# A fused four-layer kernel: attention outputs turned in pairs of head groups, elementwise steps given to GpSimd, a new order table

## The reference, cut to what matters

```python
x = x + L0_xattn(layernorm(x), ctx)      # causal, v has a bias
x = x + L0_ffn(layernorm(x))             # sign(weight)
x = x + L1_xattn(layernorm(x), ctx)      # causal
x = x + L1_ffn(layernorm(x))             # 16 experts, top 2, and 2 shared
x = x + L2_xattn(ctx, layernorm(x))      # masked; q, k, v = layernorm(linear) * scale + bias
x = x + L2_ffn(layernorm(x))             # quantised
x = x + L3_xattn(layernorm(x), ctx)      # no weights: k = v = ctx
x = x + L3_ffn(layernorm(x))             # 3 blocks of two quantised low-rank linears

# attention, for each head
weights = softmax(q @ k.T * scale); out = weights @ v
# L2_ffn: both inputs of a product are quantised
scale = 127.0 / clip(max(abs(x)), 1e-05); xq = clip(round(x * scale), -128.0, 127.0) / scale
bitlinear(x, w) = act_quant(x) @ weight_quant(w).T
out = bitlinear(silu(bitlinear(x, w_gate)) * bitlinear(x, w_up), w_down)
# L3_ffn: weight of each linear
w = (q / 7.5 - 1.0) * repeat(scale, 16); y = x @ w.T + bias + (x @ la.T) @ lb.T
```

## Time and profile before

| | us |
|---|---|
| median of 3 runs | 1191.2 |
| lowest, highest run | 1190.59, 1201.41 |
| the profiled execution | 1198.55 |
| its span, first to last instruction | 1196.6 |

### The profile page before, as it was taken

The page is one execution under the profiler, slowest core; times in us unless marked ns, Lnnn a source line. Parts: engine busy times, 40 slices in busy tenths (PEclk is TensorE's granted clock), DMA queues, the critical chain, the costliest instruction groups (busy, mean ns, idle before and its releaser), DMA issues.

```text
span 1196.6 us, 26279 instructions
## 1 busy us (share of the span) xinstructions
PE 1067.9 (89%) x8350; PEld 796.2 (67%) x8406; DVE 945.9 (79%) x3207; ACT 826.6 (69%) x1560; POOL 488.3 (41%) x1027
## 2 busy tenths in 40 slices
PE   6998999999999988899999988798899999988876
PEld 4676777777887765666677765366576766656654
DVE  3898888878555788877967798999999989898732
ACT  5777666657665666365667667457889798979953
POOL 6233356653122457657601144233334433423334
PEclk9999999999999999888999998999999999999988
DMA  7885332226777245303587752222203212121000
GB/s 221 260 275 180 87 101 71 85 76 189 218 211 213 89 121 140 85 14 116 150 259 229 233 167 80 56 69 82 82 19 87 72 54 81 53 63 54 10 10 18
DMA packets 102326, 140.03 MB, mean 117 GB/s; under 512 B 12336, under 2 KB 79792, under 8 KB 102192
## 3 DMA queue, kind: packets, MB, share of 16 engines
q1 hardware_dynamic: 99120, 129.97, 37.3%
q0 software_dynamic: 3072, 8.39, 2.2%
HBM read 65.43 MB, written 22.54 MB: 74 GB/s over the span
## 4 chain that ended last, share of the span: by engine, by line
PE 48%; DVE 20%; ACT 11%; DMA 7%; issue 6%; POOL 4%; SPq 3%; another core or an unknown queue 0%; DVEq 0%; ACTq 0%; POOLq 0%
PE ps L1516 10%; PE ps L1637 5%; PE ps L1536 4%; PE ps L1554 4%; PE ps L1729 4%; PE ps L1509 3%; DVE neg_max L2200 3%; PE ps L1523 3%; DVE ps L2196 3%; ACT probs L1945 3%; PE ps L1696 2%; DMA w<-in_expert 2%; ACT q_st L1960 2%; PE ps L1736 2%; DVE bn L2077 2%
## 5 line engine op out<-in xcount | busy, mean ns | idle before, releaser
L1945 ACT ACTIVATE probs<-ps 128x384 f32<-128x384 f32 (+1 forms) x512 | 263.5, 543 | 68.0 <-PE ps L1557 32.3
L1536 PE MATMUL ps<-k_st,q_st 96*128 96x256 bf16 (+1 forms) x1024 | 178.8, 265 | 19.4 <-DVE neg_max L2196 9.7
L1554 PE MATMUL ps<-q_st,k_st 104*128 104x256 bf16 (+1 forms) x1024 | 179.2, 263 | 14.8 <-ACT q_st L1960 6.7
L2200 DVE TENSOR_REDUCE neg_max<-ps 128x2 f32<-128x512 f32 x256 | 168.0, 679 | 11.7 <-PE ps L1536 4.9
L1960 ACT ACTIVATE q_st<-ps 8x1024 bf16<-8x1024 f32 x128 | 130.1, 1016 | 42.3 <-PE ps L1619 39.4
L2517 POOL TENSOR_SCALAR var_eps<-mv 128x2 f32<-128x2 f32 (+1 forms) x115 | 29.0, 252 | 298.0 <-DVE mv L2080 286.9
L2196 DVE CUSTOM_DVE_ANT_0 ps<-ps,diag_s 128x128 f32<-128x128 f32 (+1 forms) x384 | 123.3, 357 | 24.1 <-PE ps L1536 23.4
L1536 PEld LDWEIGHTS ps<-k_st,q_st 96*128 96x128 bf16 x1024 | 88.4, 100 | 70.3 <-DVE neg_max L2196 17.5
L1554 PEld LDWEIGHTS ps<-q_st,k_st 104*128 104x128 bf16 x1024 | 90.9, 99 | 60.3 <-issue 16.3
L1637 PE MATMUL ps<-probs,v 128*32 128x256 f32 (+1 forms) x2048 | 123.0, 359 | 4.7 <-ACT probs L1945 2.8
L2542 POOL CAST parts<-qf 128x512 bf16<-128x512 f32 x64 | 39.1, 612 | 205.2 <-DVE qf L2094 101.9
(11 more groups left out here) (270 smaller groups left out, 2545.8 us busy)
## 6 DMA issues: line engine op xcount, KB each, us to landing
k_st<-parts SPq DMA_DIRECT2D x192, 128.0 KB
q_st<-parts SPq DMA_DIRECT2D x192, 128.0 KB
w<-in_expert SPq DMA_DIRECT2D x62, 384.0 KB, 3.9
x_rows<-wo SPq DMA_DIRECT2D x10, 768.0 KB, 7.1
ctx_t<-in_ctx_t SPq DMA_DIRECT2D x16, 256.0 KB, 3.0
ring<-x_rows SPq DMA_DIRECT2D x31, 128.0 KB, 3.9
y_rows<-ring SPq DMA_DIRECT2D x31, 128.0 KB, 3.8
xn_t<-x_rows SPq DMA_DIRECT2D x31, 128.0 KB, 3.4
```

The lines of the kernel that those rows point to most:

```text
L1536: last = mm(t[:, c0:c0 + n], head(q_st, r, h, KROWS, j * P, P), head(k_st, r, h, KROWS, 0, n), start=j == 0 or L != 2, stop=L != 2, skip_g ...
L1554: last = mm(t[:, j * S:j * S + n], head(k_st, r, h, KALL, j * P, P), head(q_st, r, h, KALL, skip, n), start=j == 0 or L == 3, stop=L == 3, ...
L1945: nc.scalar.activation(probs[:, (hg % 2) * HPG + h4, 0:width], tile_of(key)[:, 0:width], ACT.Exp, scale=SCALE).then_inc(*tile_drained(key))
L2200: V.tensor_reduce(neg_max[:, hg, h4, :], tile_of(key).rearrange("p (j t) -> p j t", j=SJ), AX.X, ALU.max, negate=True).then_inc(*tile_drai ...
```

## The change

Three things change together. **Pairs:** two groups share a PSUM tile (`values` fills the left half for the even group and the right half for the odd one), one copy, four turns into one tile, one reciprocal and one product. **Steps to POOL:** the layer-2 value scale and bias, the layer-3 copy of values (`v_copy`), dequantising and scaling (`lora_scale`), and the two roundings (`quantise_round`, `hidden_round`). What reads PSUM or clips stays on DVE (`quantise_clip`, `hidden_clip`, the addition in `lora_add`). **The table** `AT` has new times in every lane.

```diff
-    (274, 278, 289, 293, 326, 330, 337, 342, 363, 367, 394, 396, 411, 424, 429, 437, 457, 460, 468, 473, 488, 511, 513, 525,
...
@@ lanes @@
     for L, b in ORDER:
-        for hg in range(HG):
+        for pair in range(HG // 2):
             yield
-            part.copy_output(L, b, hg)
+            part.copy_output(L, b, pair)
...
         part.lora(n)
         yield
+        part.lora_scale(n)
+        yield
         part.lora_add(n)
...
     part.hidden_quant(T)
     yield
+    part.hidden_round(T)
+    yield
+    part.hidden_clip(T)
+    yield
     part.down_turn(T)
...
-    part.v_take(3, b)
+    part.v_copy(3, b)
...
@@ PE @@
-                    t = claim(pe, ("o", L, b, hg))
+                    pair = ("o", L, b, hg // 2)
+                    t = (tile_of(pair) if hg % 2 else claim(pe, pair))[:, hg % 2 * S:(hg % 2 + 1) * S]
...
+                def output(L, b, pair):
+                    t = claim(pe, ("ot", L, b, pair))
+                    wait_drained(pe, ("o", L, b, pair))
                     for a in range(SJ):
-                        last = nc.tensor.transpose(t[:, a * P:(a + 1) * P], o_raw[:, hg % 2, a * P:(a + 1) * P], ident[:, :])
-                    last.then_inc(*tile_filled(("ot", L, b, hg)))
+                        for g in range(2):
+                            last = nc.tensor.transpose(t[:, (2 * a + g) * P:(2 * a + g + 1) * P], o_raw[:, g, a * P:(a + 1) * P], ident[:, :])
+                    last.then_inc(*tile_filled(("ot", L, b, pair)))
...
@@ ACT @@
+                def copy_output(L, b, pair):
+                    n = SLOT[L, b] - 1
+                    if pair:
+                        wait_filled(act, ("ot", L, b, pair - 1))
+                    elif n >= 0:
+                        wait_filled(act, ("ot", *ORDER[n], HG // 2 - 1))
+                    act.wait_ge(*pv_done.at((L, b, 2 * pair + 1)))
+                    nc.scalar.activation(o_raw[:, :, :], tile_of(("o", L, b, pair)).rearrange("p (g t) -> p g t", g=2), ACT.Copy).then_inc(
+                        *tile_drained(("o", L, b, pair)))
...
@@ DVE @@
-                    t = tile_of(key)[:, 0:SJ * P].rearrange("p (a h e) -> p a h e", a=SJ, e=DPAD)
-                    inv = sum_inv[:, hg % 2, :, :]
-                    V.reciprocal(inv, t[:, :, :, DH]).then_inc(*inverted.step((L, b, hg)))
...
+                    t = tile_of(key).rearrange("p (a h e) -> p a h e", a=SJ, e=DPAD)
+                    V.reciprocal(sum_inv[:, :, :], t[:, :, :, DH]).then_inc(*inverted.step((L, b, pair)))
...
+                def hidden_clip(T):
+                    dve.wait_ge(*hid_round.at(T))
+                    if T >= SJ:
+                        wait_filled(dve, ("ht", T - SJ))
+                    V.tensor_scalar(hid_q[:, T % SJ, :], hid[T % SJ], ROUND, Q_MAX, ALU.subtract, ALU.min).then_inc(*hid_ready.step(T))
...
@@ POOL @@
+                def value_scale(b):
+                    pool.wait_ge(*ln_done.at(("v", b, SJ - 1)))
+                    G.tensor_tensor(toks["v"], toks["v"], spread(V_L2VS, SJ), ALU.mult).then_inc(*tok_made.step(b))
...
+                def v_copy(L, b):
+                    pool.wait_ge(*pv_done.at((*same_side_before(L, b), HG - 1)))
...
+                def lora_scale(n):
+                    pool.wait_ge(*load[f"low{n}"].at(0))
+                    G.tensor_scalar(w3[:, n, :, :], w3[:, n, :, :].bitcast(I32), 1.0 / 7.5, -1.0, ALU.mult, ALU.add).then_inc(
+                        *lora_made.step(("deq", n)))
+                    pool.wait_ge(*lora_made.at(("deq", n)))
+                    pool.wait_ge(*lora_in.at((n, 3)))
+                    G.tensor_tensor(w3[:, n, :, :], w3[:, n, :, :], scale3, ALU.mult).then_inc(*lora_made.step(("mul", n)))
...
+                def quantise_round(b):
+                    flat = xn[:, NORMED["l2f"], :, :]
+                    pool.wait_ge(*quant.at(("dq_hid", b)))
...
+                def hidden_round(T):
+                    a = T % SJ
+                    h = hid[a]
+                    pool.wait_ge(*quant.at(("dqd", T)))
+                    G.tensor_scalar(h, h, hscale[:, T:T + 1], ROUND, ALU.mult, ALU.add).then_inc(*hid_round.step(T))
```

136 lines of the change are left out of this document (60 added, 76 removed), and 1060 rows, old and new, of the table AT.

## The result

The changed kernel takes 1177.6 us (median of 4 runs, 1173.1 to 1183.0), the kernel before 1195.0 beside it (median of 4); the ratio is 0.985 with an interval of 0.981 to 0.989. The forecast was 1178 us, its range 1156 to 1202; as a ratio the forecast was 0.989. The profiled execution took 1173.1 us, 1171.4 of it span. It is the fastest of the four, at a mean granted clock of 0.982; the other three, at 0.973 to 0.977, took 1175 to 1183 us. The profiled execution of the kernel before, in turn, had 0.972 and was one of its slower ones (1198.55 us), so small differences between the two profiles are read with that in mind.

The account below looks back on a forecast made before the run. PE leads with 1067.9 of 1196.6 us busy, but half the chain is other engines' work. Relief of 19.1 us, less 1.5 for hand-over and 4 for collisions, nets 13.6, taking the median from 1191.2 to 1178 us; range 1156 to 1202.

Parts of the forecast that it names:

- Loads: Expected busy times after the change: DVE about 890 us, ACT 811, POOL 552, with 17 table loads ahead of Gelu.
- The weights, 0.25 and 0.16: Share of each us of DVE and ACT relief reaching the end: 66.2 us gives 16.6, 15.7 us gives 2.5.
- Collisions and hand-over, 4 and 1.5 us: Losses charged for POOL and DVE blocking each other (4 us) and for roundings passing to POOL and back (1.5 us).
- The cover: Eight other DVE instructions, about 4.5 us, between last scalar step and clip hide POOL's rounding; without it, 24 us lost.
- The table, zero with +-9 us: New order's effect on attention end and tail: 9 us of PE work moves into the tail; taken as zero.
- the change doesn't do what it says, steps meet later than the table supposes: Rival on the order: waits sit elsewhere; not priced from rows, +-9 us its measure; 0.17 together with the held bank.
- Held bank, 1204 us: Rival: pairs hold a PSUM bank longer and PE waits, costing 26 us; 0.17 together with a table that misses.
- Full relief, 1161 us: Rival: DVE's queue sets the pace from 700 to 1148 us, so 30 of 43 us come through; chance 0.15.
- hidden anyway, 1188: Rival: PE's own order sets the time and loses no work; only table loads and scraps count; chance 0.18.

Follow-up runs that it names:

- before_small: Kernel before, old table, with VectorE's roundings and value steps done on one column only, so values are not the reference's; ratio 0.992 to the kernel before.
- before_dve2: Kernel before, old table, with each product into o_tok done twice on VectorE; ratio 1.009 to the kernel before.
- new_none: Changed kernel's new table with neither edit: groups single, the five moved functions back on VectorE; 1218.4 us, ratio 1.016 to the kernel before.
- new_moves: Changed kernel's new table with the five functions on GpSimd but groups handled one by one; 1196.3 us, ratio 1.001 to the kernel before.

## Why the prediction was right, point by point

**The number** was right, and three of its steps were not: the weights were too small, POOL's price was too small, and the table was put at nothing. The errors were of opposite sign, so that the sum came out is in part luck. That it came out to the microsecond is luck altogether: the forecast started from a median of 1191.2, the kernel before had 1195.0 beside the changed kernel, and a gain of 1.1% was forecast where 1.5% was measured (1.1 to 1.9).

*Loads.* In us of busy time: DVE 886.7 (about 890 expected), ACT 810.9 (811), POOL 554.4 (552), 17 loads ahead of Gelu (17), product 424 ns (416), PE's idle time down by 19 us (13.6). These were right. Of the unit prices the reciprocal of 16 was dearer (250 ns for 210), POOL's rounding of 1024 columns cheaper (1119 ns for 1250), that of 256 dearer (518 for 350); the late values cost 441 ns for 310, value scale and bias 1309 and 754 for 1270 and 730. The price of PE's turns was held for unchanged; they took 10 us less (below).

*The weights, 0.25 and 0.16, taken from the chain's share over busy time.* Too small: measured 0.36 to 0.46 for DVE (together 0.31 to 0.49) and 0.57, in a bad place, for ACT. The share that it was taken from is no steady number: 20% for DVE in the kernel before, 15% in before_small, 30% in before_dve2, with 2 and 3% less or more work. It tells who was last on one path of one execution. A likely reason why it falls short is that a delay of one engine moves the others that wait for it; that was not tested.

*Collisions and hand-over, 4 and 1.5 us.* The prediction expected 260 to 290 ns for each max_parts step and 10 us more of DVE. Measured are 243 and 219 ns, but the new table hides the effect: by itself it lowers the two from 477 to 453 ns together. Within one table the moved steps raised them by 15 to 30 ns together and DVE by 4 to 8 us, so the mechanism was right and its size somewhat high; on the chain stand six long max_parts steps for seven before. What was too low is the price of POOL's time as a whole: 66 us more at 0.21 are 14 us, not 4, an estimate from the doubled casts with an interval of 5 to 22. The hand-over's 1.5 us fits only the new table, where DVE never waits for the rounding. The cover was miscounted: the order shows seven DVE instructions between the last scalar step and the clip, not eight (three neg_max, not four), some 3.9 us by the changed kernel's rows for 4.5. Without cover, moving the roundings cost some 14 us; the prediction said 24 for that case, which is the right order.

*The table, zero with +-9 us.* This step failed, in what it said and in what it left out. By itself the new table is 20 us slower than the old one (new_none), and around the two edits it is worth 1.030 - 0.985, that is 54 us. The prediction costed the parts against the kernel before and added the table as a third part; yet the parts have no price apart from a table. Its rival "the change doesn't do what it says, steps meet later than the table supposes" describes the old table with the edits in it: 1234 us. Only its local reading was right: the tail grew, by 6.5 us, and the attention ended 31.7 us earlier.

*The sum by measured weights.* DVE 59.2 x 0.42 = 25, ACT 15.7 x 0.57 = 9, POOL 66 x 0.21 = 14 against: 20 us, for 18 measured. That they agree proves little, since POOL's term alone can be 5 to 22, and the table is left out. Counted from new_none, in the same table, the edits bring 38 us, and the same weights give 45.5 x 0.42 + 8.0 x 0.57 - 60.6 x 0.21 = 11 us. For the 27 us beyond the weights there are three candidates: cover that stood ready, 9 borrowings fewer, and PE's turns (below). How they share it was not separated.

*Held bank, 1204 us.* The waits of the old table fit it: 7 borrowings more, scores waiting 8 us longer, and 21 us lost where 11 us less on DVE and 6 less on ACT were by the weights worth 8, so that the pairs cost some 29 us against the rival's 26. That the bank was the cause is not shown. In the changed kernel the rival did not come, which fits the reason named against it, though not its counts: `claim` lends 18 times in the new order and 22 in the old. The prediction's 28 and 34 are near the number of PE's waits for these two banks ahead of other work than the maxima's scores, and one loan can bring more than one such wait.

*Full relief, 1161 us; hidden anyway, 1188.* The first supposed that relief comes through one to one after 700 us; of 59 us less on DVE and 16 less on ACT 18 us came through. The second falls with before_small, which gained 9.8 us by relief alone.

## What to carry to other kernels

Where in-order engines run by a written order, cost an edit together with its order: try it in the old order as well, since a relief of 46 us on VectorE, with the same edits, made this kernel 3% slower there. The first thing to look for after moving a step to another engine is the idle time ahead of the instruction that takes it back (11.2 us here without cover, 0.0 with it). And measure the weight of an engine by doubling one harmless operation: the chain's share gave 0.25 where that gave 0.36 to 0.46, and 0.16 where it gave 0.57. Keep its interval beside it, and compare the lengths of untouched instructions within one order only.

## What the runs showed of the hardware

- Four 128x128 fp32 turns in a row keep PE busy for less than two and two: 256 turns took 49.9 us in twos (also 50.4 and 49.8 in new_none and new_moves) and 39.8, 40.0 and 39.6 us in fours, 195 ns and 155 ns each. One turn is shown with 277 ns in the mean (277 to 281 over the kernels); with that a row of two takes 390 ns and a row of four 622, so each further turn adds about 115 ns (an estimate). The ends of PE's instructions are modelled by the profile, and no run tested what these 10 us were worth.
- Executions of one and the same kernel differ with the mean granted clock: of 35 runs of the kernel before, the shortest took 1189.0 us at 0.974 and the longest 1203.7 at 0.964, with a correlation of -0.85 and a slope of 0.85 us per 0.001. The program is the same in all; whether the clock makes the time or PE's waits make the clock was not tested.
- Rounding 128x1024 fp32 with one column as scale takes POOL 1.12 us and took DVE 0.83; 128x256 takes 0.52 and took 0.35. An operation with two inputs, a tile and a vector, takes POOL 1.31 us for DVE's 0.81 (128x512) and 0.75 for 0.42 (128x256).
